# Two attention layers on one core: unread passes at the start, another order at the first keys, and bias products and score rows moved

## What is computed

```python
# layer 0
q, k, v = Wq x + bq, Wk x + bk, Wv x + bv          # q, k: 32 rows, v: 256 rows
attn = softmax(q^T k, axis=-1)                      # 1024 x 1024
x = gamma * (v attn^T) + x
# layer 1
h = group_norm(x, 32 groups, eps 1e-5) * norm_w + norm_b
q, k, v = q_w h + q_b, k_w h + k_b, v_w h + v_b     # 256 rows each
attn = softmax(q^T k / 16, axis=-1)
x = x + proj_w (v attn^T) + proj_b
```

## Time and profile before

| | us |
|---|---|
| median of 3 runs | 810.87 |
| lowest and highest of them | 809.24, 812.41 |
| the profiled execution | 809.52 |
| its span, first to last instruction | 807.7 |

### The profile page before, as it was taken

One profiled execution on the slowest core, in us unless ns is written; L12 is line 12 of the kernel. 1 busy time (PEld: TensorE's weight loads), 2 busy tenths in 40 slices (PEclk: granted clock), 3 DMA queues, 4 the chain that ended last, 5 costly groups with the idle time before them and its releaser, 6 DMA issues.

```text
span 807.7 us, 9687 instructions
## 1 busy us (share of the span) xinstructions
PE 778.9 (96%) x3756; PEld 641.0 (79%) x3756; DVE 555.6 (69%) x790; ACT 468.6 (58%) x605; POOL 160.4 (20%) x144
## 2 busy tenths in 40 slices
PE   5799899999999999999999999999999999999998
PEld 4578778887788878888788877888778888887886
DVE  4855766878568785787757785577856855575564
ACT  4774764568555675557745686455855566444342
POOL 4800051023100231002310042102310024103300
PEclk9999999999999999999999999999999999999999
DMA  5100001002000030001100011000100000000101
GB/s 182 53 0 2 1 4 50 0 2 76 30 0 1 1 105 0 1 1 53 53 0 1 1 53 52 2 1 1 53 0 1 1 27 26 0 1 1 52 1 53
DMA packets 10365, 18.98 MB, mean 23 GB/s; under 512 B 2128, under 2 KB 3920, under 8 KB 10320
## 3 DMA queue, kind: packets, MB, share of 16 engines
q1 hardware_dynamic: 10320, 18.36, 6.5%
HBM read 9.97 MB, written 8.39 MB: 23 GB/s over the span
## 4 chain that ended last, share of the span: by engine, by line
PE 82%; DVE 11%; ACT 5%; issue 2%; DMA 1%; SPq 0%; ACTq 0%; DVEq 0%
PE ring L543 25%; PE ring L545 25%; PE ring L544 25%; PE ring L553 4%; PE ring L563 3%; DVE h_lo L904 2%; DVE pt_lo L1007 2%; DVE res L1043 2%; DVE q L968 1%; ACT prob L763 1%; DVE neg_raw L992 1%; ACT prob L760 1%; DVE neg_max L990 1%; ACT pt_hi L774 1%; DVE k L960 1%
## 5 line engine op out<-in xcount | busy, mean ns | idle before, releaser
L543 PE MATMUL ring<-pt_hi,v_hi 128*128 128x512 f32 x512 | 203.2, 397 | 0.6 <-DVE pt_lo L1010 0.6
L545 PE MATMUL ring<-pt_hi,v_lo 128*128 128x512 f32 x512 | 201.5, 394 | 0.0
L544 PE MATMUL ring<-pt_lo,v_hi 128*128 128x512 f32 x512 | 201.4, 393 | 0.0
L763 ACT ACTIVATE prob<-ring,neg_max 128x1024 f32<-128x1024 f32 x64 | 71.5, 1118 | 160.3 <-DVE neg_max L993 160.3
L463 POOL TENSOR_TENSOR v_lo<-v_f,v_hi 128x512 fp32r<-128x512 f32 x32 | 43.2, 1349 | 428.7 <-ACT v_hi L801 428.7
L992 DVE TENSOR_REDUCE neg_raw<-ring 128x1 f32<-128x1024 f32 x64 | 78.3, 1224 | 71.6 <-PE ring L545 71.5
L543 PEld LDWEIGHTS ring<-pt_hi,v_hi 128*128 128x128 f32 x512 | 96.9, 189 | 21.7 <-issue 1.6
L545 PEld LDWEIGHTS ring<-pt_hi,v_lo 128*128 128x128 f32 x512 | 96.8, 189 | 21.3
L544 PEld LDWEIGHTS ring<-pt_lo,v_hi 128*128 128x128 f32 x512 | 97.0, 189 | 18.8
L1007 DVE TENSOR_TENSOR pt_lo<-prob,pt_hi 128x1024 fp32r<-128x1024 f32 x64 | 83.1, 1298 | 33.1 <-ACT pt_hi L774 32.9
L990 DVE TENSOR_REDUCE neg_max<-ring 128x1 f32<-128x1024 f32 x64 | 77.8, 1222 | 37.6 <-PE ring L553 37.4
(11 more groups left out here) (133 smaller groups left out, 1218.0 us busy)
## 6 DMA issues: line engine op xcount, KB each, us to landing
out_y<-res SPq DMA_DIRECT2D x32, 256.0 KB, 2.2
x_in<-in_x SPq DMA_DIRECT2D x7, 1024.0 KB, 4.9
x_in<-in_x SPq DMA_DIRECT2D x2, 512.0 KB, 4.9
h_f<-in_wv_t SPq DMA_DIRECT2D x1, 256.0 KB, 5.2
res<-in_wq SPq DMA_DIRECT2D x1, 256.0 KB, 6.4
res<-in_wk SPq DMA_DIRECT2D x1, 256.0 KB, 6.7
res<-in_wv SPq DMA_DIRECT2D x1, 256.0 KB, 6.9
res<-in_wp_t SPq DMA_DIRECT2D x1, 256.0 KB, 7.0
```

Of the source, the lines that this page charges most:

```text
L543: mm(out, w_hi, m_hi, start=first, stop=False)
L544: mm(out, w_hi, m_lo, start=False, stop=False)
L545: return mm(out, w_lo, m_hi, start=False, stop=last)
L763: activation(prob[:, p % PROBS], ring[:, slot], ACT.Exp, bias=neg_max[:, k % 2:k % 2 + 1], accum_out=row_sum[:, k % 2:k % 2 + 1]).then_inc ...
```

## The change

Seven edits:

1. TensorE, once `ones` is written, first does 30 matmuls of `ones` by `ones` into slot 3 (128 columns, float32), which nobody reads (`keep_busy`).
2. SP issues the two bias vectors of `wqk` after the two halves of image 0, on a semaphore of their own; VectorE's split of `wqk` no longer waits for them.
3. In the opening VectorE makes the shift before it takes the keys of image 1; ScalarE takes its part of both halves in `steps[0]`, behind the first `prob` and `pt_hi`.
4. POOL waits for the shift before it writes `bv_rows` and `bq_rows`.
5. `("value0", 0, 2)` goes behind the product of the shift.
6. The bias products go from `steps[5]` of image 0 (slot 0) to `s10`, behind `keys` 1 of image 1 (slot 3); VectorE takes them before `pt_lo` of that tile, and `s2` begins with two banks of values.
7. `scores` 0 to 2 of image 2 go from `early` to `late` in `s5` to `s7`, `value0` 1 of image 2 from `s6` to `s7`, more banks stand ahead of the sides, and in `s4` VectorE makes `pt_lo` before it takes the `qk` (`low_first`).

```diff
-PLACE = {("qk", 1, 0): 2, ("value0", 0, 2): 3, ("bias", 0, 0): 0}
+PLACE = {("qk", 1, 0): 2, ("value0", 0, 2): 3, ("bias", 0, 0): 3}
...
-    opening.sides = tiles("qk", 1, (0, 1)) + tiles("value0", 0, (2,))
-    opening.late = tiles("shift", 0, (0,))
+    opening.sides = tiles("qk", 1, (0, 1))
+    opening.late = tiles("shift", 0, (0,)) + tiles("value0", 0, (2,))
...
-    steps[5].sides = tiles("bias", 0, (0,))
...
+    s10.sides = tiles("bias", 0, (0,))
...
-    s2.banks_first = 0
+    s2.banks_first = 2
...
+    s4.banks_first = 3
     s4.sides = tiles("qk", 2, (1,)) + tiles("norm", 0, (0,))
-    s5.early = tiles("scores", 2, (0,))
+    s4.low_first = True
+    s5.banks_first = 2
     s5.sides = tiles("value0", 2, (0,)) + tiles("norm", 0, (1,))
-    s6.early = tiles("scores", 2, (1,))
-    s6.sides = tiles("value0", 2, (1,))
+    s5.late = tiles("scores", 2, (0,))
+    s6.late = tiles("scores", 2, (1,))
     s6.hidden = s7.hidden_lo = 0
-    s7.early = tiles("scores", 2, (2,))
+    s7.banks_first = 4
+    s7.sides = tiles("value0", 2, (1,))
+    s7.late = tiles("scores", 2, (2,))
...
-                    ("wqk_loaded", ((wqk_f, by_tile(wqk_t)), (bqk_s[:], bqk), (bk0_s[:], bk0))),
+                    ("wqk_loaded", ((wqk_f, by_tile(wqk_t)),)),
...
+                    ("bqk_loaded", ((bqk_s[:], bqk), (bk0_s[:], bk0))),
...
             first_split_x()
+            pool.wait_ge(S["shift_ready"], 1)
             bias_rows()
...
+            def keep_busy(out, passes):
+
+                for _ in range(passes):
+                    mm(out[:, 0:P], ones[:], ones[:], start=True, stop=True)
...
+            wait("ones_ready", 1)
+            keep_busy(ring[:, 3], 30)
             for now in STEPS:
...
                 shift_rows(("shift", 0, 0))
-                key_part(("qk", 1, 0))
...
                 if now.rest:
-                    key_part(("qk", 1, 1))
+                    for m in range(2):
+                        key_part(("qk", 1, m))
...
             def opening():
-                key_part(("qk", 1, 0))
                 shifts(0)
-                key_part(("qk", 1, 1))
+                for m in range(2):
+                    key_part(("qk", 1, m))
```

More of the change, by code:

```diff
@@ L45, in __init__ @@
         self.statistics = self.evacuate = self.evacuate_at_once = None
-        self.take_weights = self.opening = self.rest = False
+        self.take_weights = self.opening = self.rest = self.low_first = False
     def entries(self):
         return [self.tile] * bool(self.tile) + self.early + self.sides + self.late
-PLACE = {("qk", 1, 0): 2, ("value0", 0, 2): 3, ("bias", 0, 0): 0}
+PLACE = {("qk", 1, 0): 2, ("value0", 0, 2): 3, ("bias", 0, 0): 3}
 PLACE.update({("weights", 0, m): 3 for m in range(4)})
@@ L258 @@
     "layer0_split", "v0_weights", "small_ready", "ones_ready", "key_hi", "link", "pool_link",
-    "wqk_loaded", "wv0_loaded", "weights_loaded", "x_loaded0", "x_loaded1", "x0_loaded", "y_stored")
+    "wqk_loaded", "bqk_loaded", "wv0_loaded", "weights_loaded", "x_loaded0", "x_loaded1", "x0_loaded", "y_stored")
 def build(nc, x, wqk_t, bqk, bk0, wv0_t, bv0, gamma, norm_w, norm_b, wq, bq, wk, bk, wv, bv, wp_t, bp,
@@ L817, in query_part @@
                 _, i, m = entry
+                if i == 0 and m == 0:
+                    act.wait_ge(S["bqk_loaded"], 16 * 2)
                 act.wait_ge(S["ring_ready"], RING_NO[entry] + 1)
@@ L907, in first_weights @@
             def first_weights():
-                dve.wait_ge(S["wqk_loaded"], 16 * 3)
+                dve.wait_ge(S["wqk_loaded"], 16)
                 split(wqk_hi[:], wqk_lo[:], wqk_f).then_inc(S["layer0_split"], 1)
@@ L957, in key_part @@
                 _, i, m = entry
+                if i == 0 and m == 0:
+                    dve.wait_ge(S["bqk_loaded"], 16 * 2)
                 dve.wait_ge(S["ring_ready"], RING_NO[entry] + 1)
@@ L1086, in _ @@
                     shifts(now.early_log)
-                first = [entry for entry in now.sides if entry[0] in ("qk", "norm")]
+                first = [entry for entry in now.sides if entry[0] in ("qk", "norm", "bias")]
+                if now.low_first:
+                    prob_lo(now.tile)
                 for entry in first:
-                    if entry[0] == "qk":
+                    if entry[0] != "norm":
                         follow(entry)
@@ L1097, in _ @@
                         split_x(*now.x_lo_mid)
-                elif now.tile:
+                elif now.tile and not now.low_first:
                     follow(now.tile)
```

## The result

The changed kernel takes **804.11 us** (median of 4 runs, 804.08 to 804.83), against 811.14 for the kernel before in the same session (4 runs, 809.24 to 812.41). The ratio is 0.9936, with an interval of 0.9920 to 0.9952: faster, by more than 0.5% on the middle value, though the interval's upper end stops at 0.48%. The profiled execution took 804.08 us with a span of 802.3; the one before had 807.7. So 5.4 us of span are to be found.

What follows compares the result with a forecast made beforehand. TensorE, busy 96% of the span, bounds the kernel and loses time in the first 110 us. Terms 1.1 + 2.7 + 2.05 - 0.55 = 5.3 us off 809.5 give 804.2; with half the median's offset 804.8 us, range 801.5 to 808.2.

Steps and rivals of the forecast that it cites:

- The start: Up to the first scores: full-clock `qk` matmuls, less the delay by the passes, gain 1.1 us (0.6 to 1.55).
- Rival D: At the start, passes don't overlap their weight loads: first real matmul at 16.9 instead of 9.8, 811.9 us; chance 6%.
- The opening: Way to image 1's first keys: earlier shift without POOL's work beside it, gain 2.7 us, ends 2.0 and 3.2.
- This is hidden: Opening: half clock after TensorE's longer wait costs nothing, because the third keys wait for ScalarE and VectorE anyway.
- The bias products: Moved from `steps[5]` to `s10`: gain 4.8 us there, loss 2.75 here, sum 2.05, ends 0.5 and 3.75.
- 1.7 for the half clock: In `s10`, behind the bias products' new place: TensorE runs at half clock, 1.7 us of the 2.75 loss.
- rival B's first half: TensorE keeps its clock behind the bias products (1.7 us); with `keys` 7's exponential done (1.7), 801.4; whole rival's chance 12%.
- Edit 7: Order around image 2: gains 0.95 and 0.2, new wait before `scores` 2 costs 1.7, net loss 0.55 us.
- `scores` 1 ends at 3.2, VectorE's maximum at 4.5: Image 2, us from the end of `keys` 6: chain to the exponential at 9.1, TensorE arriving at 7.9, 1.3 lost.
- Rival A: New places eat the gain: image 2's order costs 1.6 us, bias products bring only 0.5; 807.4 us, chance 16%.
- Rival C: At `pt_lo` of tile 1, VectorE waits for one whole POOL operation, 1.19 us; 806.0 us, chance 8%.
- my argument against the wait: `pt_lo` at 110.93, beside POOL, took 1.64 us in all; a full wait would leave only 0.45 for the operation.

Runs made afterwards that it cites:

- the two kernels beside it: Two variants of the changed kernel: 20 instead of 30 passes, 804.19 us; the bias vectors of `wqk` back in front of image 0, 804.43 us.

## Why the prediction held, and where it didn't

The forecast, 804.8 with 801.5 to 808.2, held: 804.11, faster. The sum of 5.3 us was right to 0.1, but its terms weren't.

**The start** was predicted to gain 1.1 and gained 0.59. The passes made room at 10.01, within 9.5 to 10.4; a pass cost 0.43 us at the low and 0.225 at the full clock, against my 0.45 and 0.225 (30 passes in 9.28 us, 11 of them at the low clock). What failed is the second half of the step. I let VectorE's six operations and the first six matmuls take 6.15 us; from the first matmul to the first scores it is 16.62 - 10.01 = 6.61. VectorE's six operations took 4.59 as predicted (4.56). But it began 1.76 behind the first matmul (11.77) instead of 1.45, since the first of the six took 0.32 and the last must run through before VectorE reads it; and TensorE started 0.26 behind VectorE's end (16.36) instead of 0.14. Rival D is out: the weight loads overlap.

**The opening** was predicted as 2.7 and gave 3.12, with its working right: shift at 28.49, small operations at 0.17 us, the second `prob` 3.71 us earlier, 3.1 of it the opening's own (predicted 2.9). The second key part added 0.58 to ScalarE's chain and not 0.71, and the 0.2 taken off for POOL's later work didn't appear. "This is hidden", said of the half clock behind TensorE's longer wait, held: it is felt at `keys` 3 and gone at `scores` 2 of image 1. Undone alone, edit 4 costs 2.4 and edit 3 1.2. That the medians lose more when they are undone (4.5, 2.8, and 4.6 for all three) is the half clock in open places of those executions, and with edit 4 the later start, which the sum didn't have.

**The bias products** were predicted as 2.05, with 0.5 and 3.75 as ends, and gave 3.70, the upper end. Of the two halves, leaving `steps[5]` gave 8.60 - 3.71 = 4.9 us (`keys` 0 of image 1 came at 74.56 instead of 83.16), where I had 4.8; coming back in `s10` cost 8.60 - 7.41 = 1.2, where I had 2.75, or 1.05 without its half clock. The step that failed is "1.7 for the half clock": TensorE kept 1.00 from 77 to 84. This is rival B's first half, which I had given too little. It isn't a property of the place: in the profiled executions of eight other kernels with the products in the same place half clock did follow, from about 78.5 on in one to 84.4 in another, and in three it didn't. With it `keys` 2 to `keys` 3 of image 1 last 6.3 us, without it 4.7, so it is worth 1.6 us, and executions of one kernel differ by about that. The first kernel without passes had two such stretches in a row. The same holds of the gain: 1.3 of the 3.70 are the half clock that this execution of the kernel before had in the old place, where the kernel with edit 6 undone had none.

**Edit 7** was predicted as a loss of 0.55 and lost 1.85, just beyond its end of 1.6. The gain before `value0` 0 was right: 0.39 left of 1.55, 1.16 gained (predicted 0.95). The wait before `scores` 2 came as predicted, 1.50 us for 1.7. The step that failed is the line "`scores` 1 ends at 3.2, VectorE's maximum at 4.5". I counted VectorE as free there and corrected it by 0.4 to 0.8 for a slower `pt_lo`; in fact the maximum started when ScalarE's `pt_hi` let `pt_lo` go, 5.7 us behind the last one, and TensorE waited 1.30 us for it before `value0` 1, in a place where I had booked a gain of 0.2. Rival A, that the new places eat the gain, came true for this edit and failed for the other.

**Rival C** didn't come true in the kernel after: `pt_lo` of tile 1 took 1.22 us at 38.36, because POOL's cast started behind it, at 38.83. But my argument against the wait was wrong. In all profiles every `pt_lo` of layer 0 over 1.35 us issued 0.12 us or more behind the start of an operation of POOL and ended 1.06 to 1.09 us behind the end of that operation, so it waited for all that was left of it: `pt_lo` of tile 0 (33.98, 1.56 us) ends at 35.54, POOL's cast of 0.62 us (33.84) at 34.46; the one at 192.46 issued 0.15 us behind an operation of 1.21 and took 2.13; and the row of 1.64 at 110.93 in the kernel before ends at 112.57, 1.07 behind POOL's 111.50. I had compared with a whole operation, where only 0.57 us of it were left. Without edit 3 `pt_lo` of tile 1 did meet this wait (38.90, 1.78 us), at a price of half a us.

**What the scatter says.** The executions of a changed kernel differ by up to 3.3 us, those of the kernel before by 5 (808.13 to 813.09 in one group), and traces show two sources: the length of 30 passes (8.75 to 9.88 us in different executions, as 8 to 14 of them ran at the low clock) with what it moves, and whether half clock follows the bias products. I found no quantity in the rows that tells which it will be: first scores at 15.35, 16.10 and 17.22 had it, 15.49, 16.62 and 17.15 had not. This stays open. The total was thus right partly by chance: with half clock behind the products the same kernel would have shown a gain near 3.8 us of span.

## What to carry to other kernels

Before a short operation of an engine on the critical path, look at what another engine does on the same memory: 0.17 us became 1.72, and one wait on the engine that had time gave back 2.4 us. Before moving an entry to the end of a step, follow it once around all in-order engines: if the maximum stands behind an operation that itself waits for the last maximum, the step lasts as long as this loop, whatever TensorE does. Warming passes should end when the data arrives (22 here, not 30), and a sum that comes out right is no evidence for its terms; compare the marks between, and look for a loss seen at one mark again at the next, since it can be made up by then.

## What the runs showed of the hardware that I had not expected

- **Half clock moves instead of going away.** Filled at one wait, it followed the next one (42.8 to 46.2), and with the bias products back in `steps[5]` it stood at 81.8 to 88.6. Two stretches of 3.4 us often come as one of 6.5 to 7 (36.8 to 43.3 in the kernel after; 78.8 to 85.6 without passes). One costs 1.6 us where TensorE is the bound, and two in a row cost nothing where ScalarE and VectorE lead.
- **Passes at the head seem to matter beyond the start.** Without them the start is 0.22 us later, yet the median is 2.1 us higher, and in the profiled execution the loss lies 60 us behind the passes. That its 7 runs lie above all 8 of the two kernels beside it is shown; where the loss lies is one profile, and why it does so isn't shown.
- **A cast of 128x8 took 1.72 us beside POOL's operations** and 0.17 without them. A `pt_lo` of 128x1024, with two inputs, waits for the rest of POOL's operation under way: it took 1.56, 1.78 and 2.13 us instead of 1.22. The exclusion works the other way too: POOL's operation behind the first of them took 2.13 us (34.54) where one of the same shape without VectorE beside it took 1.19 (37.31).
